# A two-block network head on one core: finer gathers from one scratch tensor, and merged products in a small convolution

## The reference

```
x = x + displace(group_norm(x), offset)     # 32 groups of 12 channels
x = x + hadamard(group_norm(x))             # over the channels
```

## Time and profile before

| | us |
|---|---|
| median of 3 runs | 284.46 (283.58 to 286.48) |
| the profiled execution | 283.06 |
| its span, first to last instruction | 281.4 |

### The profile page before, as it was taken

How to read it: one execution, slowest core, us unless ns; L and a number is a source line. 1 busy time by engine, 2 the same in 40 slices (tenths; PEclk the granted TensorE clock), 3 DMA queues, 4 the chain that set the end, 5 groups by cost and what they waited for, 6 DMA issues and landing times.

```text
span 281.4 us, 2494 instructions
## 1 busy us (share of the span) xinstructions
PE 156.2 (56%) x742; PEld 98.1 (35%) x742; DVE 201.3 (72%) x313; ACT 128.3 (46%) x189; POOL 35.7 (13%) x52
## 2 busy tenths in 40 slices
PE   0000000054971698299700589999988982899710
PEld 0000000044961698299600524444333331243200
DVE  0899999986761892577530337999999980899950
ACT  1003999929810410131000199988886603993000
POOL 0000000000000563335433600000000220000000
PEclk9999999999985599779955558999999997599995
DMA  5999999999991168997640662139999999457798
GB/s 183 417 409 409 410 409 410 311 374 410 300 250 36 23 170 195 244 279 212 146 145 22 212 273 96 76 112 408 345 360 375 390 365 402 172 233 292 292 404 346
DMA packets 25278, 76.80 MB, mean 273 GB/s; under 512 B 7368, under 2 KB 7624, under 8 KB 25048
## 3 DMA queue, kind: packets, MB, share of 16 engines
q1 hardware_dynamic: 18928, 67.07, 66.8%
q0 software_dynamic: 5504, 9.51, 10.6%
q10 hardware_dynamic: 832, 0.05, 0.2%
HBM read 67.07 MB, written 29.99 MB: 345 GB/s over the span
## 4 chain that ended last, share of the span: by engine, by line
DMA 48%; DVE 25%; issue 7%; ACT 6%; PE 4%; SPq 2%; POOL 2%; POOLq 1%; DVEq 0%; ACTq 0%
DMA ring<-x_pad 28%; DVE ring L908 14%; DMA stat_rows<-blk_stat 6%; DVE parts L264 6%; DMA ring<-x_from,row_at 6%; DMA blk<-x_pad 5%; DMA out<-ring 4%; ACT blk L500 3%; ACT parts L508 2%; PE ps L555 2%; POOL x_from L273 2%; PE ps L542 1%; DVE blk L264 1%; PE ps L533 1%; DVE blk L814 1%
## 5 line engine op out<-in xcount | busy, mean ns | idle before, releaser
L614 PE MATMUL ps<-parts,had_sb 128*128 128x512 f16 x216 | 56.2, 398 | 6.8 <-DVE parts L264 4.4
L908 DVE SCALAR_TENSOR_TENSOR ring<-ps,beta,ring 128x1024 f32<-128x1024 f32 x48 | 59.6, 1273 | 0.0
L542 PE MATMUL ps<-geo_sb,blk 128*128 128x128 f32 x72 | 13.6, 357 | 71.5 <-DMA blk<-x_pad 56.7
L555 PE MATMUL ps<-parts 128*128 128x64 f32 (+4 forms) x306 | 42.1, 305 | 6.5 <-ACT parts L454 6.4
L555 PEld LDWEIGHTS ps<-parts 128*128 128x128 f32 x306 | 41.5, 219 | 7.2 <-ACT parts L454 6.8
L264 DVE TENSOR_TENSOR parts<-blk,parts 128x1024 f16<-128x1024 f32 x27 | 32.7, 1213 | 15.3 <-ACT parts L508 15.3
L753 DVE BATCH_NORM_STATS2 halfstat<-ring 128x6 f32<-128x512 f32 x64 | 38.9, 670 | 4.9 <-DMA ring<-x_pad 4.9
L500 ACT ACTIVATE blk<-ring,gn 128x1024 f32<-128x1024 f32 x32 | 37.7, 1227 | 0.0
L624 PE MATMUL ps<-ring,first_w 128*128 128x512 f32 x64 | 34.4, 664 | 5.7 <-ACT first_w L492 5.7
L542 PEld LDWEIGHTS ps<-geo_sb,blk 128*128 128x128 f32 x72 | 11.6, 189 | 72.0 <-issue 65.3
L614 PEld LDWEIGHTS ps<-parts,had_sb 128*128 128x128 f16 x216 | 20.6, 101 | 44.4 <-DVE parts L264 12.4
(11 more groups left out here) (109 smaller groups left out, 125.5 us busy)
## 6 DMA issues: line engine op xcount, KB each, us to landing
ring<-x_pad SPq DMA_DIRECT2D x20, 1536.0 KB, 15.3
out<-ring SPq DMA_DIRECT2D x13, 1536.0 KB, 7.3
blk<-x_pad SPq DMA_DIRECT2D x18, 512.0 KB, 8.2
out<-ring SPq DMA_DIRECT2D x9, 512.0 KB, 5.2
x_from<-blk POOLq DMA_DIRECT2D x9, 288.0 KB, 4.1
x_from<-blk POOLq DMA_DIRECT2D x9, 128.0 KB, 4.8
x_from<-blk POOLq DMA_DIRECT2D x9, 96.0 KB, 3.9
geo_sb<-geo SPq DMA_DIRECT2D x1, 683.0 KB, 4.7
```

The costliest lines, as they stand in the source:

```text
L542: last = pe.transpose(pixels[:, j // 4, 128 * (j % 4):128 * (j % 4 + 1)], shifted[:, 128 * j:128 * (j + 1)], eye)
L555: last = pe.matmul(sums[:, bank, 32 * (a - 16 * bank):32 * (b - 16 * bank)], pixels[:, j, :], weights[:, a - (4 * j - 1):b - (4 * j - 1), ...
L614: last = pe.matmul(ps[n % 4][:, h, :], had_sb[:, sign, :], part_of(n, t, part)[:, 512 * h:512 * (h + 1)], start=False, stop=ends and part ...
L908: dve.scalar_tensor_tensor(ring[:, m, place_of(i), :], ps[n % 4][:, :, :].rearrange("p a n -> p (a n)"), beta[:, i % BATCH:i % BATCH + 1], ...
```

## The change

The three scratch tensors become one, `x1_rows`, with a row of 16 images for each compact channel. `leave` writes a block with one DMA, and a buffer is free after two DMAs instead of four (`blk_out` counts to 32 for 64). The gathers go over seven parts instead of three: images 4 to 7, 8 to 11, 12 to 15, and images 0, 1, 2, 3 one by one. A gather sees `x1_rows` as rows of 4 images (or of 1), so each part has an index table of its own, filled by seven small VectorE instructions at the end of the slot parameters; POOL waits for them (`rows_ready`). Each reload has its own semaphore, and POOL gathers image j as soon as reload j has landed. ACT waits at n = 0, 4, 8 and then at each of 12, 13, 14, 15.

`convolve_block` makes one product per chunk and bank over all the rows that the chunk touches there, so 10 in a block; the first of a bank still has `start=True`, and rows that it did not write are written first by a later product.

```
-PARTS = ((4, 3), (7, 9), (0, 4))
+PARTS = [(4, 4), (8, 4), (12, 4)] + [(j, 1) for j in range(EXTRA)]
+KEPT = 3
...
-    x1_part = {first: nc.dram_tensor(f"x1_from{first}", [CHANNELS, count * PIXELS], FP32).ap() for first, count in PARTS}
+    x1_rows = nc.dram_tensor("x1_rows", [CHANNELS, BATCH * PIXELS], FP32).ap()
...
-        row_at = sb("row_at", [128, CT], INT32)
+        row_at = sb("row_at", [128, len(PARTS), CT], INT32)
...
-        reload_done = sem("reload_done")
-        patch_done = [sem(f"patch_done{part}") for part in range(2)]
-        late_patch_done = sem("late_patch_done")
+        reload_done = [sem(f"reload_done{j}") for j in range(EXTRA)]
+        rows_ready = sem("rows_ready")
+        part_in = [sem(f"part_in{n}") for n in range(len(PARTS))]
...
-        def rows_out(eng, row, count, tile, sem):
-
-            for first, count in PARTS:
-                eng.dma_start(x1_part[first][row, :].rearrange("c (b n) -> b c n", n=PIXELS),
-                              tile[BIND * first:BIND * (first + count), :]).then_inc(sem, 16)
-
-        def gather_rows(eng, first, count, limit, signal):
-
-            rows, at = x1_part[first], place_of(first + BATCH) if first < EXTRA else place_of(first)
+        def gather_part(eng, n, limit, signal):
+
+            first, count = PARTS[n]
+            at = place_of(first + BATCH) if first < EXTRA else place_of(first)
+            runs = x1_rows[0:limit, :].rearrange("c (g n) -> (c g) n", n=count * PIXELS)
             for t in range(CT):
                 eng.indirect_dma_start(ring[:, t, at:at + count, :].rearrange("p b n -> p (b n)"), None,
-                                       rows[0:limit, :], bass.IndirectOffsetOnAxis(ap=row_at[:, t:t + 1], axis=0),
-                                       bounds_check=limit - 1, oob_is_err=False).then_inc(signal, 16)
+                                       runs, bass.IndirectOffsetOnAxis(ap=row_at[:, n, t:t + 1], axis=0),
+                                       bounds_check=limit * BATCH // count - 1, oob_is_err=False).then_inc(signal, 16)
...
                 if k >= DEEP:
-                    sp.wait_ge(blk_out[k % DEEP], 64 * (k // DEEP))
+                    sp.wait_ge(blk_out[k % DEEP], 32 * (k // DEEP))
...
-                sp.dma_start(ring[:, :, j, :], x_bcp[j]).then_inc(reload_done, 16)
+                sp.dma_start(ring[:, :, j, :], x_bcp[j]).then_inc(reload_done[j], 16)
...
                 pool.wait_ge(x1_done, k + 1)
-                rows_out(pool, slice(BIND * k, BIND * (k + 1)), BIND, blk[:, u, :], blk_out[u])
+                pool.dma_start(x1_rows[BIND * k:BIND * (k + 1), :].rearrange("c (b n) -> b c n", b=BATCH), blk[:, u, :]).then_inc(blk_out[u], 16)
...
+            pool.wait_ge(rows_ready, 1)
...
-            for part, (first, count) in enumerate(PARTS[0:2]):
-                gather_rows(pool, first, count, FAST * BIND, patch_done[part])
-            pool.wait_ge(reload_done, 16 * EXTRA)
-            first, count = PARTS[2]
...
-            gather_rows(pool, first, count, FAST * BIND, late_patch_done)
+            for n in range(KEPT):
+                gather_part(pool, n, FAST * BIND, part_in[n])
+            for j in range(EXTRA):
+                pool.wait_ge(reload_done[j], 16)
...
+                gather_part(pool, KEPT + j, FAST * BIND, part_in[KEPT + j])
...
-            act.wait_ge(patch_done[0], 16 * CT)
             for n in range(BATCH):
-                if n == PARTS[0][1]:
-                    act.wait_ge(patch_done[1], 16 * CT)
-                if n == RING:
-                    act.wait_ge(late_patch_done, 16 * CT)
+                part = n // EXTRA if n < RING else KEPT + n - RING
+                if n % EXTRA == 0 or n >= RING:
+                    act.wait_ge(part_in[part], 16 * CT)
...
                 for bank in range(2):
-                    seen = 16 * bank
                     for j in range(3 * bank, 3 * bank + 5):
                         lo = max(4 * j - 1, 16 * bank)
                         hi = min(4 * j + 5, 16 * bank + 16)
-                        for a, b in ((lo, seen), (seen, hi)):
-                            if a < b:
-                                last = pe.matmul(sums[:, bank, 32 * (a - 16 * bank):32 * (b - 16 * bank)],
-                                                 pixels[:, j, :], weights[:, a - (4 * j - 1):b - (4 * j - 1), :],
-                                                 start=(j == 3 * bank), stop=(j == 3 * bank + 4 and b == hi))
-                        seen = hi
+                        last = pe.matmul(sums[:, bank, 32 * (lo - 16 * bank):32 * (hi - 16 * bank)],
+                                         pixels[:, j, :], weights[:, lo - (4 * j - 1):hi - (4 * j - 1), :],
+                                         start=(j == 3 * bank), stop=(j == 3 * bank + 4), skip_group_check=True)
...
-            dve.tensor_scalar(row_at[:, :], row_f[:, 1, :], geo_sb[:, G_LANE:G_LANE + 1], None, ALU.add).then_inc(rank_done, 1)
+            dve.tensor_scalar(row_f[:, 0, :], row_f[:, 1, :], geo_sb[:, G_LANE:G_LANE + 1], None, ALU.add).then_inc(rank_done, 1)
...
             slot_parameters(slot_ids(0, FAST), FAST, link, place_done, exp_in, exp_done, 1, conv_w_done)
+
+            for n, (first, count) in enumerate(PARTS):
+                last = dve.tensor_scalar(row_at[:, n, :], row_f[:, 0, :], float(BATCH // count), float(first // count), ALU.mult, ALU.add)
+            last.then_inc(rows_ready, 1)
```

More of the change, by code:

```diff
@@ L267, in fast_blocks_out @@
             for u in range(DEEP):
-                eng.wait_ge(blk_out[u], 64 * blocks_in(u))
-        def rows_out(eng, row, count, tile, sem):
-            for first, count in PARTS:
-                eng.dma_start(x1_part[first][row, :].rearrange("c (b n) -> b c n", n=PIXELS),
-                              tile[BIND * first:BIND * (first + count), :]).then_inc(sem, 16)
-        def gather_rows(eng, first, count, limit, signal):
-            rows, at = x1_part[first], place_of(first + BATCH) if first < EXTRA else place_of(first)
+                eng.wait_ge(blk_out[u], 32 * blocks_in(u))
+        def gather_part(eng, n, limit, signal):
+            first, count = PARTS[n]
+            at = place_of(first + BATCH) if first < EXTRA else place_of(first)
+            runs = x1_rows[0:limit, :].rearrange("c (g n) -> (c g) n", n=count * PIXELS)
             for t in range(CT):
                 eng.indirect_dma_start(ring[:, t, at:at + count, :].rearrange("p b n -> p (b n)"), None,
-                                       rows[0:limit, :], bass.IndirectOffsetOnAxis(ap=row_at[:, t:t + 1], axis=0),
-                                       bounds_check=limit - 1, oob_is_err=False).then_inc(signal, 16)
+                                       runs, bass.IndirectOffsetOnAxis(ap=row_at[:, n, t:t + 1], axis=0),
+                                       bounds_check=limit * BATCH // count - 1, oob_is_err=False).then_inc(signal, 16)
         def fetch_gn(eng, k):
@@ L342, in _ @@
                 for u in range(DEEP):
-                    sp.wait_ge(blk_out[u], 64 * blocks_in(u))
+                    sp.wait_ge(blk_out[u], 32 * blocks_in(u))
                 with sp.Fori(FAST, OFFSETS) as k:
@@ L354, in _ @@
                     sp.wait_ge(more_ready, m + 1)
-                    rows_out(sp, ds(k * BIND, BIND), BIND, blk[:, 0, :], more_out)
+                    sp.dma_start(x1_rows[ds(k * BIND, BIND), :].rearrange("c (b n) -> b c n", b=BATCH), blk[:, 0, :]).then_inc(more_out, 16)
                     sp.dma_start(stat_rows[ds(c_at, BIND), :].rearrange("c (b k) -> b c k", k=2), blk_stat[:, 0, :]).then_inc(more_out, 16)
@@ L415, in _ @@
             with pool.If(active > FAST):
-                pool.wait_ge(more_out, 64 * (OFFSETS - FAST))
+                pool.wait_ge(more_out, 32 * (OFFSETS - FAST))
             pool.dma_start(stat[:, :, :, :].rearrange("p t b k -> p t (b k)"),
                           stat_rows.rearrange("(t c) n -> c t n", t=CT)).then_inc(stat_patched, 16)
+            pool.wait_ge(rows_ready, 1)
             with pool.If(active > FAST):
-                for first, count in PARTS[0:2]:
-                    gather_rows(pool, first, count, CHANNELS, more_patched)
-                pool.wait_ge(more_patched, 16 * 2 * CT)
-            for part, (first, count) in enumerate(PARTS[0:2]):
-                gather_rows(pool, first, count, FAST * BIND, patch_done[part])
-            pool.wait_ge(reload_done, 16 * EXTRA)
-            first, count = PARTS[2]
-            with pool.If(active > FAST):
-                gather_rows(pool, first, count, CHANNELS, more_patched)
-                pool.wait_ge(more_patched, 16 * 3 * CT)
-            gather_rows(pool, first, count, FAST * BIND, late_patch_done)
+                for n in range(KEPT):
+                    gather_part(pool, n, CHANNELS, more_patched)
+                pool.wait_ge(more_patched, 16 * CT * KEPT)
+            for n in range(KEPT):
+                gather_part(pool, n, FAST * BIND, part_in[n])
```

(10 more changed lines are left out.)

## The result

The changed kernel took 268.59 us, median of 4 runs (267.72 to 270.10), where the kernel before took 284.02 in the same comparison (283.27 to 286.48). The ratio is 0.9448, with a 95% interval from 0.9375 to 0.9521. The medians differ by 15.4 us, 11.45 were forecast; the profiled executions differ by 13.0 us in their spans (281.4 and 268.4).

A forecast was written before the change was run, and what follows sets the result against it. VectorE bounds the output stage, with one hole; a ring of three buffers bounds the convolution. 9.21 + 2.6 + 0.9 - 1.26 = 11.45 us off 283.06 gives 271.6, plus 1.4 for the median: 273.0 us, range 269 to 275.5.

The forecast's parts named there:

- The hole: Output stage: VectorE waits from 231.2 to 240.4 us for late gathers; gathering reload by reload gains 9.2 us.
- The rival that the stores take over: Output stage: stores, with the DMA share already 1.00, end after VectorE: 276 us, chance 0.18.
- The first part: Start of output stage: the gather releasing ACT holds four images instead of three, cost 1.26 us.
- The writing of a block: Convolution stage: one POOL issue replaces three; statistics issued sooner (1.7) and landing sooner (0.9), gain 2.6 us.
- the landing: Statistics behind a block's write land sooner as rows enter the queue earlier: 0.3 us each passage, ends 0 and 1.2.
- The products: Convolution, block 5: 20 records instead of 34 per block, 3.1 us for 3.98; gain 0.9 us.
- slower rival: TensorE stays at 1.2 GHz in the convolution, having more pauses: 288.2 to 300.8 us, chance 0.03; partial 0.04.

The follow-up runs named there:

- late single write: The changed kernel, but POOL issues a block's single write only after VectorE's aggregate: 274.43 us, 5.6 slower than the changed kernel.
- all pieces back: The changed kernel with the 17 products per block of before in all blocks: 271.83 us, 4.6 us slower than the changed kernel.
- 20 products ahead: The kernel before with 20 float16 products, results never read, between transposes and products of the first two blocks: 285.15 us for 284.65.

## Why the prediction fell short

**The hole (9.2 us): right.** The output stage shrank by 9.3 us, and its length was the same 110.8 in nearly every trace with these gathers. The rival that the stores take over did not come about: the tail is 10.3 us as before. (Its price had been worked out loosely: half of 3 to 6 us on top of 273.0 gives 274.5 to 276, and against a forecast of 273.0 a time of 276 leaves 6.2 of the 9.2 us, not 5.4.)

**The first part (1.3 us of cost): right.** The releasing gather took 7.25, 5.76 and 6.40 us in three traces of the changed kernel, 6.5 on average against 5.40. Over all traces with four images in the part it is 6.45 us (ten traces, 5.74 to 7.31), with three images 5.3 (three traces, 4.95 to 5.45): 1.2 us for the 1.26 forecast.

**The writing of a block (2.6 us): mis-sized and put in the wrong place.** Three writes again cost 5.1 us, about twice my sum. Of the 1.7 us by which the statistics should be issued sooner, about 0.5 came. POOL takes 0.67 us from the end of VectorE's aggregate to the issue (127.34 to 128.01), not 0.28, and before the change it had been 0.80, 1.07 and 0.69 us behind it in blocks 0, 5 and 8, so it had hardly waited for its three issues. What I had put at 0.3 us a passage, the landing, gave 2.4 and 1.6 in two passages of the first pair of traces and nothing in the first one. The late single write shows why the landing is what matters: the statistics land some 2 us behind the rows, so what makes the rows leave sooner is gained, whenever the statistics are issued. I had the bound for that, 1.2 us a passage, and chose near its lower end. With it in all three passages the term would have been 3.6 + 0.5 = 4.1 us.

**The products (0.9 us): the failed step.** "For the other blocks PE is not last, and it costs nothing and brings nothing" held for the one execution that I read, and not for the kernel. For block 5 the term was right in the first pair of traces (0.7 us). But all pieces back cost 4.6 us, and merging alone took 1.8 us off the median of the kernel before. In one trace the pieces of blocks 0 and 1 were 3.6 us late for the first normalisation; in the earlier trace rows the group sums at 78.56 stood directly behind the pieces, so there had been about nothing to spare, which I did not look at. In two others block 8's products at half clock ended last (5.93 us merged, 7.69 in pieces). This is my slower rival's mechanism, present in both kernels for single blocks, and merging makes it cheaper. (The price of that rival in full was 2 us too high: at 97.5 us block 2's transposes are already done.)

**The median.** The sum was made against one execution and 1.4 us were added. The kernel before scatters over 8 to 10 us in a set (278.6 to 291.1 in all), the changed one over 2 to 3. A single profile of such a kernel can't give a sum good to 2 us.

**What stays open.** The share of the early and of the late blocks in the 4.6 us: pieces in the two early blocks alone cost 1.4 us, not clear of noise; pieces in the seven late ones 1.3 to 2.9 us by the medians of other sets, and as much as all pieces by the ratio. Whether three writes cost because the last rows leave late or because of how they are spread; the single write was never tried on the kernel before by itself. And where all of the scatter of the kernel before comes from: the experiment that should have removed it at its supposed source did not. The effects of the parts (9.3 for the hole, 5.1 and 4.6 for what was undone, less 1.1) add up to 17.9, more than 15.4, so they overlap. With the 1.8 us that merging brought to the kernel before, the sum is 15.1.

## What to carry to other kernels

- Where a small transfer behind a large one frees a buffer, issue the large one as early as it can be; 1.8 us of delay per block cost 5.6 us here, with three passages on the path.
- Before calling an engine's work free, look for the queue directly behind it, price it at the half clock, and ask how many us are to spare.
- Where a wait covers several pieces, cut it at what the consumer needs first: the wait and the size of the first piece each held about half of this hole.

## What the runs showed of the hardware

The granted clock of a stretch reads 1.00 ahead of the first recorded change, whatever it was. The same 68 records took 15.04, 11.94 and 11.81 us in three traces in which the table says 1.00 for them, and 12.67 us in the one with the 20 products ahead, whose record begins earlier and says 0.60 (67.4 to 80 us). Their four records of 160 columns averaged 528 ns where the table says 1.00 (kernel before) and where it says 0.50 (20 products ahead), and 300 ns later at full clock. In that last trace the clock was full while the 20 products ran at 224 ns and at half when the pieces began, after 2.4 us of pause. A small write issued 0.6 or 1.9 us behind a 512 KB write of the same engine landed some 2 us behind it in both cases (1.0 to 3.2 us in four traces; in the two with a semaphore of its own for the statistics, 0.2 to 3.7). And the third gather of four images took between 5.76 and 7.25 us in three executions of one kernel, a spread as large as what one image more costs in it.
